# The last batch's values and keys beside the heads of the batch before it, and the first batch's gates among the second batch's front

## The chip, the cores and the metric

One core of a Trainium2 chip runs the program. The metric is the device time of one execution in microseconds (us); lower is better. The engines are PE (matrix products), DVE (vector), ACT (activations), POOL (GpSimd) and SP (it issues DMAs). Each works through its own list of instructions strictly in order, and they wait for one another through semaphores. PE reads SBUF and writes eight PSUM banks of 128x512 f32.

## The reference

`x` is 8 batches of 512 tokens with 128 channels, all f32. Each batch goes through two layers, each with two halves, every half a layer norm with scale and shift, then a residual add:

```
x += ga * attn0(norm(x))   # 16 heads, linear attention with elu, then a dense MLP with gelu
x += gb * moe(norm(x))     # 8 experts, each 128 -> 512 -> 128, silu(x Wg) * (x Wu) Wd
x += ga * attn1(norm(x))   # 8 causal heads of 16, softmax, within the 512 tokens
x += gb * switch(norm(x))  # 16 heads of 64, softmax over 512 tokens
# switch: gates Ws, Wd (16 heads x 8 experts), top 2 of 8 for each token and head
#   values v = sum of 2 experts' projections, weighted by sigmoid of the gate (mix_v)
#   q, k dense; attn = softmax(q k) v; result = sum over heads and 2 experts of attn @ Wo
```

The 512 tokens are four tiles of 128. Batches don't depend on each other.

## The kernel before

Each batch passes these stages, written on every engine as generators that yield "marks" (the count of marks in brackets):

- FRONT_A: `load` (1), `attn0` (24), `moe_in` (3): first layer's attention, MLP and the norm ahead of the experts. A long chain of short operations that hand over from engine to engine.
- `experts` (32): one mark for each block of 128 hidden units; three PE products, an ACT silu and a DVE product.
- FRONT_B: `attn1` (48, of which 35 are its 32 head tiles) and `gates` (13): the top-2 choice on `gate` with DVE and POOL on 128x1024 f32 tiles `eq`, `cand`, `oh1`, `oh2`; it ends in `mixv` (POOL) and `masko` (DVE).
- `values` (33): PE projects four tiles `pv` (experts' values) and eight blocks of `keys`; ACT copies them out of PSUM. 32 pieces then multiply `pv` with `mixv` into `prod` (three buffers, `NPROD`), and DVE sums each piece into `vals`. The products are shared between POOL and DVE: `VALUES_V` gives DVE every fourth, `LAST_VALUES_V` every second for the last batch. POOL's product n waits for the sum n-3; DVE's sum n waits for product n and stands one mark behind it.
- `begin` (2): the first two blocks of queries. `heads` (83): 64 head tiles and, between them, queries, `back`, `mixed` and `result` steps. For each pair of heads PE writes scores to banks S0 and S1, DVE takes the negated row maximum (`nmax`, L1520), ACT the exponential (`pr`, L1195), PE transposes into TB, ACT copies to `prT` (L1182), PE multiplies with `vals` into OB. `finish` (5) and `close` (4): the last tile's way through a DRAM round trip (`out_rows`, `onR`) to `xout` and the output DMA.

`schedule` merges two lists of marks for every engine alike: a main list, and a list beside it that is spread evenly over it (a mark of attn1's head tiles counts 1/4 to 1 by its width, the others 1, finish 1.6). `program` gives this order, with b the loop's batch:

1. FRONT_A(0); experts(0); FRONT_B(0); then FRONT_A(1) and experts(1) with values(0), begin(0) beside them.
2. Loop, six times: heads(b-1) with attn1(b), then gates(b) woven into FRONT_A(b+1) beside it; then experts(b+1) with finish(b-1), values(b), close(b-1), begin(b) beside it.
3. heads(6) with attn1(7), gates(7) beside; then finish(6), values(7), close(6), begin(7) with nothing beside; then heads(7), finish(7), close(7).

`arena` is a scratch tile of 128x6144 f32 that all stages up to attn1 share. `hdT` is the normed input of the switch layer, `hdB` its copy, made because the next front overwrites hdT; `xout` begins as a copy of `x5` for the like reason. values(b) uses banks TB, OB, S0, S1, which heads also use; the fronts and experts use F0 to F3.

Of the kernel before, what the change touches and what calls it, by code (L numbers as in the profile page):

```python
# [52 lines left out]
LAST_VALUES_V = [n for n in range(NQ * NT) if n % 2]  # L53


def values_v(b):
    return LAST_VALUES_V if isinstance(b[0], int) and sum(b) == NB - 1 else VALUES_V

# [47 lines left out]
CLOSE_BEHIND, BEGIN_BEHIND = 4, 28  # L106

# [17 lines left out]
def build(nc, a, row_table, out):  # L125
    ctx = ExitStack()
    with ctx:
# [104 lines left out]
        eq = sb("eq", [P, 2 * NT * HS, NE])[:, :, :]  # L232
        cand = sb("cand", [P, 2 * NT * HS, NE])[:, :, :]
        oh1 = sb("oh1", [P, 2 * NT * HS, NE])[:, :, :]
        oh2 = sb("oh2", [P, 2 * NT * HS, NE])[:, :, :]
# [9 lines left out]
        vals = sb("vals", [P, NT, HS, DS])  # L245
# [3 lines left out]
        keys = sb("keys", [P, NP, T])  # L249
# [17 lines left out]
        F0, F1, F2, F3, S0, S1, TB, OB = bank  # L267

# [133 lines left out]
        stage = vals[:, :, :, :].rearrange("p i h d -> p (i h d)")[:, 0:8 * T].rearrange("p (a t) -> p a t", a=8)  # L402
# [116 lines left out]
        def _(sp):  # L519
# [42 lines left out]
            def values(b):  # L562
                wait(sp, masko_r, b, 1)
                sp.dma_start(mask_rows.rearrange("(i p) c -> p i c", p=P), masko[:, :, :, :].rearrange("p i h e -> p i (h e)")).then_inc(mask_out[0], 16)
                yield CLOSE_BEHIND
                wait(sp, mask_out, b, 16)
                sp.dma_start(maskR[:, :, :], mask_rows.rearrange("(n t) (h e) -> (t h) n e", t=TG, e=NE)).then_inc(mask_in[0], 16)
                yield NQ * NT // 2
# [145 lines left out]
        def _(pe):  # L714
# [197 lines left out]
            def values(b):  # L912

                wait(pe, pT_r, b, 0)
                wait(pe, oa_r, b, 0)
                for n in range(NQ * NT):
                    if n == 0:
                        for i in range(2):
                            pe.matmul((TB, OB)[i][:, :], hdT[:, i * P:(i + 1) * P], WvT[:, :], start=True, stop=True).then_inc(pv_ps[0], 1)
                    if n % NQ == 0 and n // NQ in (1, 2):  # L920
                        i = n // NQ + 1
                        if i == 2:
                            wait(pe, s_out, b, 0)
                            wait(pe, xout_r, b, 0)
                        pe.matmul((S0, S1)[i % 2][:, :], hdT[:, i * P:(i + 1) * P], WvT[:, :], start=True, stop=True).then_inc(pv_ps[0], 1)
                    if n % 4 == 2:
                        p = n // 4
                        if p < 2:
                            wait(pe, hdB_r, b, 1)
# [3 lines left out]
                        pe.matmul((TB, OB)[p % 2][:, :], WkT[:, p * P:(p + 1) * P], hdB[:, :], start=True, stop=True).then_inc(k_ps[0], 1)  # L933
                    yield n + 1

            def begin(b):
                wait(pe, pv_r, b, NT)
# [24 lines left out]
            def steps(b, first, end):  # L962


                for k in range(first, end):
# [7 lines left out]
                    if kind == "queries":  # L973
                        for p in range(4):
                            last = pe.matmul(bank_k[:, p * P:(p + 1) * P], WqT[:, (4 * (x % 2) + p) * P:(4 * (x % 2) + p + 1) * P], hdB[:, (x // 2) * P:(x // 2 + 1) * P], start=True, stop=True)
# [29 lines left out]
                    if kind == "head":  # L1005
                        wait(pe, s_out, b, COPIED[k - 2])
                        if m >= 1:
# [24 lines left out]
        def _(s):  # L1032
# [105 lines left out]
            def values(b):  # L1138
                wait(s, vals_r, b, 0)
                for n in range(NQ * NT):  # L1140
                    if n == 0 or n % NQ == NQ // 2:
                        for i in (0, 1) if n == 0 else (n // NQ + 1,) if 1 <= n // NQ < NT - 1 else ():
# [3 lines left out]
                            s.activation(pv[:, i % 2, :], (TB, OB, S0, S1)[i][:, :], ACT.Copy).then_inc(pv_r[0], 1)  # L1146
                    if n % 4 == 3:
                        p = n // 4
                        wait(s, k_ps, b, p + 1)
                        s.activation(keys[:, p, :], (TB, OB)[p % 2][:, :], ACT.Copy).then_inc(keys_r[0], 1)  # L1150
                    if n == 0:
                        s.activation(hdB[:, :], hdT[:, :], ACT.Copy).then_inc(hdB_r[0], 1)
                    if n == NQ * NT // 2:
# [17 lines left out]
            def steps(b, first, end):  # L1171
                for k in range(first, end):
# [15 lines left out]
                    if kind == "head":  # L1188
# [4 lines left out]
                        if h == 0 and i >= 2:  # L1193
                            wait(s, rden_r, b, 2 * (i - 1))
# [16 lines left out]
        def _(v):  # L1211
# [257 lines left out]
            def values(b):  # L1469
                wait(v, mix_g, b, 3)  # L1470
                wait(v, oa_r, b, 0)
# [19 lines left out]
            def heads(b):  # L1491
                wait(v, xcopy_r, b, 1)
# [8 lines left out]
            def steps(b, first, end):  # L1501
                for k in range(first, end):
                    kind, m, _ = step_of(k - 1)
                    if kind == "result":
                        wait(v, s_ps, b, TURN[k - 1])
                        v.tensor_tensor(xout[:, m, :], (S0, S1)[TURN[k - 1] % 2][:, 0:P], xout[:, m, :], ALU.add).then_inc(xout_r[0], 1)
# [54 lines left out]
```

## Time and profile before

| | |
|---|---|
| median of 3 runs | 3037.46 us (3032.28 to 3060.35) |
| the profiled execution | 3036.23 us, of which 3034.4 us span from first to last instruction |
| PE busy | 2497.6 us, 82% of the span |
| DVE busy | 1565.5 us, 52% |
| ACT busy | 1361.4 us, 45% |
| POOL busy | 803.4 us, 26% |
| mean granted PE clock | 0.924 of 2.4 GHz |

The busy shares are means over stages with different limits; the profiled execution's own time is 1.8 us over its span, and 1.2 us under the median. A change in one stage is to be read from that stage's stretch of the trace.

### The profile page before, as it was taken

To read this page: it belongs to the slowest core of one execution; us is meant where nothing else is said; L and a number is where in the kernel's file an instruction comes from. 1 tells how busy PE (TensorE), PEld (TensorE's weight loads), DVE (VectorE), ACT (ScalarE), POOL (GpSimd) and SP (SyncE) were. 2 spreads that over 40 slices of the span, in tenths; PEclk is the share of its full clock that TensorE was granted. 3 is DMA by queue.
4 is the path that set the end of the run, shared out by engine and by line. 5 is a ranking of instruction groups with operands and counts; after the bars stand their busy time and mean duration, and the time that the engine had idled before them with its cause. 6 is when DMAs were issued, how large, how long until landed. Compare 5 with 4: busy or idle time off the path is not lost.

```text
span 3034.4 us, 45348 instructions
## 1 busy us (share of the span) xinstructions
PE 2497.6 (82%) x15660; PEld 1535.7 (51%) x15660; DVE 1565.5 (52%) x2646; ACT 1361.4 (45%) x2925; POOL 803.4 (26%) x370
## 2 busy tenths in 40 slices
PE   3984699879897898889898798978988898986476
PEld 2353346554475445654365544754456544754254
DVE  4235753456635484464835565364834557337632
ACT  0232226463364525554265634555255633643254
POOL 1002620015501191013700164011900147004500
PEclk7996799999899998999899998999989999998798
DMA  2110010102010030102101030101201121001001
GB/s 75 42 49 9 9 54 1 50 22 67 22 38 20 25 78 2 43 28 47 44 1 56 15 77 12 43 15 43 60 2 43 29 56 33 15 15 40 0 29 32
DMA packets 210741, 101.69 MB, mean 34 GB/s; under 512 B 137369, under 2 KB 189622, under 8 KB 210494
## 3 DMA queue, kind: packets, MB, share of 16 engines
q1 hardware_dynamic: 205052, 95.74, 11.4%
q10 hardware_dynamic: 5440, 2.75, 0.3%
q8 instruction: 143, 2.34, 0.3%
q14 instruction: 106, 0.85, 0.1%
HBM read 77.48 MB, written 20.99 MB: 32 GB/s over the span
## 4 chain that ended last, share of the span: by engine, by line
issue 42%; PE 34%; POOL 10%; DVE 7%; ACT 6%; DMA 1%; ACTq 0%; POOLq 0%; DVEq 0%
POOL prod L702 7%; PE bank L717 6%; PE bank L984 5%; PE bank L829 4%; PE bank L832 4%; PE bank L1021 3%; PE bank L837 3%; ACT prT L1182 2%; ACT pr L1195 2%; POOL rstd L641 1%; PE bank L869 1%; DVE nrm_o L1294 1%; PE bank L996 1%; DVE prod L1477 1%; PE bank L885 1%
## 5 line engine op out<-in xcount | busy, mean ns | idle before, releaser
L702 POOL TENSOR_TENSOR prod<-pv,mixv 128x1024 f32<-128x1024 f32 x184 | 608.3, 3344 | 243.3 <-ACT pv L1146 170.5
L1520 DVE TENSOR_REDUCE nmax<-bank 128x1 f32<-128x512 f32 x512 | 340.6, 687 | 608.1 <-PE bank L984 605.6
L1182 ACT ACTIVATE prT<-bank 128x512 f32<-128x512 f32 x512 | 305.6, 597 | 611.2 <-PE bank L717 607.3
L984 PE MATMUL bank<-keys,qs 64*128 64x512 f32 x1024 | 318.0, 698 | 220.1 <-ACT pr L1195 92.4
L641 POOL TENSOR_TENSOR rstd<-vareps,minus_half 128x4 f32<-128x4 f32 x48 | 50.0, 1042 | 1323.7 <-DVE vareps L1289 1323.6
L1195 ACT ACTIVATE pr<-bank,nmax 128x512 f32<-128x512 f32 x512 | 349.5, 685 | 98.3 <-DVE nmax L1520 97.3
L717 PE MATMUL bank<-ident,pr 128*128 128x128 f32 x2048 | 351.7, 298 | 36.1 <-ACT prT L1182 35.9
L717 PEld LDWEIGHTS bank<-ident,pr 128*128 128x128 f32 x2048 | 241.8, 150 | 270.1 <-issue 217.1
L1088 ACT ACTIVATE arena<-bank 128x512 f32<-128x512 f32 x256 | 152.8, 597 | 469.3 <-PE bank L829 429.4
L1021 PE MATMUL bank<-prT,vals 128*64 128x128 f32 x4096 | 299.5, 292 | 63.0 <-ACT prT L1182 63.0
L1485 DVE TENSOR_REDUCE vals<-prod 128x128 f32<-128x1024 f32 x256 | 306.6, 1208 | 35.9 <-POOL prod L702 35.9
L1378 DVE TENSOR_TENSOR arena<-bank,arena 128x512 f32<-128x512 f32 x256 | 175.1, 686 | 245.2 <-PE bank L832 230.9
L1021 PEld LDWEIGHTS bank<-prT,vals 128*64 128x64 f32 x4096 | 235.8, 145 | 115.4 <-ACT prT L1182 72.7
L832 PE MATMUL bank<-h1T,Wu 128*128 128x512 f32 x512 | 268.4, 606 | 19.0 <-DVE arena L1378 19.0
L1406 DVE TENSOR_REDUCE nmax<-bank 128x1 f32<-128x128 f32 (+3 forms) x256 | 125.7, 491 | 282.9 <-PE bank L870 282.2
L829 PE MATMUL bank<-h1T,Wg 128*128 128x512 f32 x512 | 266.2, 602 | 0.9 <-ACT h1T L1053 0.9
L837 PE MATMUL bank<-arena,Wd 128*128 128x512 f32 x512 | 263.6, 600 | 2.8 <-DVE arena L1378 2.4
L984 PEld LDWEIGHTS bank<-keys,qs 64*128 64x128 f32 x1024 | 84.3, 197 | 281.3 <-ACT pr L1195 113.2
L869 PE MATMUL bank<-arena,attT 128*128 128x512 f32 (+3 forms) x512 | 198.9, 473 | 4.4 <-ACT arena L1116 3.0
L1477 DVE TENSOR_TENSOR prod<-pv,mixv 128x1024 f32<-128x1024 f32 x72 | 179.7, 2495 | 0.0
L832 PEld LDWEIGHTS bank<-h1T,Wu 128*128 128x128 f32 x512 | 97.6, 193 | 147.1 <-issue 113.2
L885 PEld LDWEIGHTS bank<-v,arena 128*128 128x128 f32 x1280 | 165.8, 194 | 1.0 <-issue 1.0
(220 smaller groups left out, 3077.1 us busy)
## 6 DMA issues: line engine op xcount, KB each, us to landing
Wg<-in_L_ffn_Wg SPq DMA_DIRECT2D x64, 256.0 KB, 2.8
Wu<-in_L_ffn_Wu SPq DMA_DIRECT2D x64, 256.0 KB, 3.1
Wd<-in_L_ffn_Wd SPq DMA_DIRECT2D x64, 256.0 KB, 3.8
out_rows<-on SPq DMA_DIRECT2D x32, 512.0 KB, 2.6
onR<-out_rows SPq DMA_DIRECT2D x32, 512.0 KB, 3.8
xin<-in_L_attn_x SPq DMA_DIRECT2D x8, 256.0 KB, 4.2
mask_rows<-masko SPq DMA_DIRECT2D x8, 256.0 KB, 4.3
maskR<-mask_rows SPq DMA_DIRECT2D x8, 256.0 KB, 6.6
```

The costliest lines, as they stand in the source:

```text
L702: g.tensor_tensor(*value_piece(n), ALU.mult).then_inc(vprod_r[0], 1)
L717: last = pe.transpose(dst[:, i * P:(i + 1) * P], src(i), ident[:, :])
L829: pe.matmul(F0[:, :], Wg[:, e % 2, j * P:(j + 1) * P], hbT[:, :], start=True, stop=True).then_inc(gu_g[0], 1)
L832: pe.matmul((F2, F3)[n % 2][:, :], Wu[:, e % 2, j * P:(j + 1) * P], hbT[:, :], start=True, stop=True).then_inc(gu_u[0], 1)
L837: pe.matmul(F1[:, :], Wd[:, e % 2, j, :], act[:, m % 3, :], start=(m == 0), stop=(m == n_all - 1)).then_inc(down_ps[0], 1)
L869: pe.matmul(f[:, 0:w], q1T[:, i * P:(i + 1) * P], k1z[:, h, 0:w], start=True, stop=False, skip_group_check=True)
L984: pe.matmul((S0, S1)[(turn + odd) % 2][:, :], qs[half, j % 3, r, :], keys[half, p, :], start=True, stop=True).then_inc(s_ps[0], 1)
L1021: last = pe.matmul(OB[DS * odd:DS * odd + DS, at:at + P], vals[:, j, h - 1 + odd, :], prT[:, (m - 1 + odd) % 3, j * P:(j + 1) * P], start= ...
L1182: s.activation(prT[:, m % 3, :], TB[:, :], ACT.Copy).then_inc(pT_r[0], 1)
L1195: s.activation(pr[:, x % 2, :], bank_k[:, :], ACT.Exp, bias=nmax[:, x % 2:x % 2 + 1], accum_out=den[:, i % 2, h:h + 1]).then_inc(s_out[0], 1)
L1485: v.tensor_reduce(vals[:, i, HQ * q:HQ * q + HQ, :], prod[:, m % NPROD, :].rearrange("p (h d e) -> p h d e", h=HQ, e=NE), X_AXIS, ALU.add) ...
L1520: v.tensor_reduce(nmax[:, m % 2:m % 2 + 1], (S0, S1)[turn % 2][:, :], X_AXIS, ALU.max, negate=True).then_inc(nmax_r[0], 1)
```

## The change

The last batch's values and keys get memory and banks of their own, so that values(7) can run while heads(6) still read theirs: `vals` of batch 7 lies in arena[0:4096], which attn1 of that batch has by then left; `keys` of batch 7 lies in the memory of eq, cand, oh1, oh2 (now one tile `picks`), free once masko and mixv are made. The products go to banks F0 to F3. The copies hdB and xout are left out for that batch. DVE's share of its products falls from 16 to 10 of 32. In `program`, marks 1 to 24 of values(7) stand behind attn1(7) and gates(7) beside heads(6), 25 to 28 beside finish(6), 29 to 32 beside close(6), mark 33 with begin(7). At the start, gates(0) is woven into FRONT_A(1) behind attn1(0), with nothing beside, and values(0), begin(0) stand beside experts(1) alone.

```
-LAST_VALUES_V = [n for n in range(NQ * NT) if n % 2]
+LAST_VALUES_V = [n for n in range(NQ * NT) if n % 3 == 2]
+LAST_BESIDE = 24
-        vals = sb("vals", [P, NT, HS, DS])
-        keys = sb("keys", [P, NP, T])
+        vals_last = arena[:, 0:NT * HS * DS].rearrange("p (i h d) -> p i h d", i=NT, h=HS)
+        keys_last = picks[:, :, :, :].rearrange("p k n e -> p (k n e)").rearrange("p (a t) -> p a t", a=NP)
...
-                              (of(FRONT_B, 0), []), (of(FRONT_A, 1) + of(("experts",), 1), of(("values", "begin"), 0))])
+                              (fronts(0), []), (of(("experts",), 1), of(("values", "begin"), 0))])
...
-            schedule(stages, [(of(("heads",), last - 1), of(FRONT_B, last)),
-                              (after_heads(last, -1), []), (of(("heads", "finish", "close"), last), [])])
+            at = (last, 0)
+            schedule(stages, [(of(("heads",), last - 1), of(FRONT_B, last) + [("values", at, range(1, LAST_BESIDE + 1))]),
+                              (of(("finish",), last - 1), [("values", at, range(LAST_BESIDE + 1, LAST_BESIDE + CLOSE_BEHIND + 1))]),
+                              (of(("close",), last - 1), [("values", at, range(LAST_BESIDE + CLOSE_BEHIND + 1, MARKS["values"]))]),
+                              (of(("begin",), last) + [("values", at, [MARKS["values"]])], []),
+                              (of(("heads", "finish", "close"), last), [])])
...
+                if is_last(b):
+                    A, B, C, D, of_hd = F0, F1, F2, F3, hdT
+                    wait(pe, gate_r, b, 2)
+                else:
+                    A, B, C, D, of_hd = TB, OB, S0, S1, hdB
...
             def begin(b):
-                wait(pe, pv_r, b, NT)
+                if is_last(b):
+                    wait(pe, s_out, b, 0)
+                    wait(pe, xout_r, b, 0)
+                    wait(pe, oa_r, b, 0)
+                else:
+                    wait(pe, pv_r, b, NT)
...
+                        if p == 0 and is_last(b):
+                            wait(s, masko_r, b, 1)
+                            wait(s, mix_g, b, 3)
...
             def heads(b):
-                wait(v, xcopy_r, b, 1)
+                if is_last(b):
+                    wait(v, stored, b, 0)
+                else:
+                    wait(v, xcopy_r, b, 1)
```

## Rows read from the trace of the kernel before

**Rows 1.** Windows: width; busy (count) PE, PEld, DVE, ACT, POOL; PE clock; DMA share; GB/s

```profile
284.00:361.00 77.00, 31.93 (x83) 17.27 (x84) 61.61 (x99) 12.54 (x21) 52.14 (x22) 0.66 0.06 4
361.00:450.00 89.00, 88.98 (x220) 39.55 (x218) 47.05 (x52) 24.80 (x41) 27.79 (x11) 1.00 0.17 54
2447.00:2555.00 108.00, 103.91 (x336) 47.98 (x335) 79.54 (x76) 31.85 (x54) 81.38 (x25) 0.98 0.24 62
2767.00:2848.00 81.00, 28.63 (x152) 16.57 (x147) 74.11 (x54) 11.80 (x22) 70.48 (x17) 0.63 0.13 24
```

**Rows 2.** Timeline of DVE: front(0) begins; gates(0); front(1) begins; heads(0) begin

```profile
42.79 0.87 DVE L1281 BATCH_NORM_STATS2 stats<-xin 128x6 f32<-128x128 f32 x4 [5.41 <-DMA rows<-row_table]
...
263.15 1.22 DVE L1434 TENSOR_REDUCE top<-gate 128x128 f32<-128x1024 f32 x1 [6.55 <-ACT gate L1130]
...
284.56 0.17 DVE L1300 TENSOR_SCALAR modA<-mod 128x12 f32<-128x12 f32 x1 [3.22 <-POOL mixv L692]
...
450.42 0.69 DVE L1520 TENSOR_REDUCE nmax<-bank 128x1 f32<-128x512 f32 x1 [2.88 <-PE bank L984]
```

**Rows 3.** Timeline of PE: the first Wg product of experts(0) and (1)

```profile
94.67 2.08 PE L829 MATMUL bank<-h1T,Wg 128*128 128x512 f32 x2 [0.93 <-ACT h1T L1053]
...
360.58 1.06 PE L829 MATMUL bank<-h1T,Wg 128*128 128x512 f32 x1
```

**Rows 4.** Timeline of DVE: a norm's four tiles in batch 0's, then batch 1's front

```profile
91.46 1.11 DVE L1294 TENSOR_SCALAR nrm_o<-h,mv,rstd 128x128 f32<-128x128 f32 x4 [1.13 <-POOL rstd L641]
...
323.96 8.06 DVE L1294 TENSOR_SCALAR nrm_o<-h,mv,rstd 128x128 f32<-128x128 f32 x4 [1.12 <-POOL rstd L641]
```

**Rows 5.** L1520's busy us (count), PE clock, in windows of heads(5), (6), (7)

```profile
2207.50:2338.00 130.50, 20.89 (x31) 0.94 0.08 25
...
2720.20:2766.70 46.50, 10.73 (x18) 0.85 0.08 24
2847.60:2925.90 78.30, 19.94 (x32) 0.96 0.05 15
2925.90:2958.20 32.30, 7.13 (x13) 1.00 0.12 33
2958.20:3011.00 52.80, 13.55 (x21) 0.97 0.07 21
2969.00:3011.00 42.00, 10.35 (x17) 0.96 0.09 26
```

**Rows 6.** Products in 2447:2555, then 2787:2848: duration ns min/median/max, first, last start

```profile
L702 POOL TENSOR_TENSOR prod<-pv,mixv x24: 2822/2856/4497, 2465.9 to 2546.2; 128x1024 f32<-128x1024 f32 x24
...
L1477 DVE TENSOR_TENSOR prod<-pv,mixv x8: 1926/2772/3309, 2473.3 to 2549.0; 128x1024 f32<-128x1024 f32 x8
...
L702 POOL TENSOR_TENSOR prod<-pv,mixv x13: 4332/4350/4406, 2787.6 to 2839.4; 128x1024 f32<-128x1024 f32 x13
...
L1485 DVE TENSOR_REDUCE vals<-prod x29: 1197/1207/1216, 2786.3 to 2846.5; 128x128 f32<-128x1024 f32 x29
```

**Rows 7.** Timeline of one pair of heads of batch 7

```profile
2972.15 1.29 DVE L1520 TENSOR_REDUCE nmax<-bank 128x1 f32<-128x512 f32 x2 [2.50 <-PE bank L984]
...
2974.68 0.68 ACT L1195 ACTIVATE pr<-bank,nmax 128x512 f32<-128x512 f32 x1
```

**Rows 8.** Timeline of DVE: heads(6) begin; its tail; heads(7) begin; its tail

```profile
2555.02 0.69 DVE L1520 TENSOR_REDUCE nmax<-bank 128x1 f32<-128x512 f32 x1 [1.22 <-PE bank L984]
...
2774.22 4.43 DVE L1477 TENSOR_TENSOR prod<-pv,mixv 128x1024 f32<-128x1024 f32 x1
...
2847.61 0.68 DVE L1520 TENSOR_REDUCE nmax<-bank 128x1 f32<-128x512 f32 x1
3010.41 1.29 DVE L1520 TENSOR_REDUCE nmax<-bank 128x1 f32<-128x512 f32 x2 [1.28 <-PE bank L984]
...
3017.96 0.69 DVE L1514 TENSOR_TENSOR on<-bank,rden 128x512 f32<-128x512 f32 x1 [4.75 <-PE bank L988]
...
3031.50 0.29 DVE L1506 TENSOR_TENSOR xout<-bank,xout 128x128 f32<-128x128 f32 x1 [11.72 <-PE bank L1002]
```

More of the change, by code:

```diff
@@ L52, with is_last @@
 VALUES_V = [n for n in range(NQ * NT) if n % 4 == 3]
-LAST_VALUES_V = [n for n in range(NQ * NT) if n % 2]
+LAST_VALUES_V = [n for n in range(NQ * NT) if n % 3 == 2]
+def is_last(b):
+    return isinstance(b[0], int) and sum(b) == NB - 1
 def values_v(b):
-    return LAST_VALUES_V if isinstance(b[0], int) and sum(b) == NB - 1 else VALUES_V
+    return LAST_VALUES_V if is_last(b) else VALUES_V
 def by_pool(n, by_v):
@@ L231, in build @@
         gate = sb("gate", [P, 2, NT, HS, NE])
[L232 to L235, printed above, removed]
+        picks = sb("picks", [P, 4, 2 * NT * HS, NE])
+        eq, cand, oh1, oh2 = (picks[:, k, :, :] for k in range(4))
         top = sb("top", [P, 2, 2 * NT * HS])
@@ L267, in build, with vals_of, keys_of @@
         F0, F1, F2, F3, S0, S1, TB, OB = bank
+        def vals_of(b):
+            return vals_last if is_last(b) else vals_loop
+        def keys_of(b):
+            return keys_last if is_last(b) else keys_loop
         def tiles(t):
@@ L564, in values @@
                 sp.dma_start(mask_rows.rearrange("(i p) c -> p i c", p=P), masko[:, :, :, :].rearrange("p i h e -> p i (h e)")).then_inc(mask_out[0], 16)
-                yield CLOSE_BEHIND
+                yield MARKS["values"] - 1 if is_last(b) else CLOSE_BEHIND
                 wait(sp, mask_out, b, 16)
                 sp.dma_start(maskR[:, :, :], mask_rows.rearrange("(n t) (h e) -> (t h) n e", t=TG, e=NE)).then_inc(mask_in[0], 16)
-                yield NQ * NT // 2
+                if not is_last(b):
+                    yield NQ * NT // 2
                 wait(sp, xout_r, b, 0)
@@ L918, in values @@
                         for i in range(2):
-                            pe.matmul((TB, OB)[i][:, :], hdT[:, i * P:(i + 1) * P], WvT[:, :], start=True, stop=True).then_inc(pv_ps[0], 1)
+                            pe.matmul((A, B)[i][:, :], hdT[:, i * P:(i + 1) * P], WvT[:, :], start=True, stop=True).then_inc(pv_ps[0], 1)
                     if n % NQ == 0 and n // NQ in (1, 2):
                         i = n // NQ + 1
-                        if i == 2:
+                        if i == 2 and not is_last(b):
                             wait(pe, s_out, b, 0)
                             wait(pe, xout_r, b, 0)
-                        pe.matmul((S0, S1)[i % 2][:, :], hdT[:, i * P:(i + 1) * P], WvT[:, :], start=True, stop=True).then_inc(pv_ps[0], 1)
+                        pe.matmul((C, D)[i % 2][:, :], hdT[:, i * P:(i + 1) * P], WvT[:, :], start=True, stop=True).then_inc(pv_ps[0], 1)
                     if n % 4 == 2:
@@ L928, in values @@
                         if p < 2:
-                            wait(pe, hdB_r, b, 1)
+                            if not is_last(b):
+                                wait(pe, hdB_r, b, 1)
                             wait(pe, pv_r, b, p + 1)
@@ L932, in values @@
                             wait(pe, keys_r, b, p - 1)
[L933 removed]
+                        pe.matmul((A, B)[p % 2][:, :], WkT[:, p * P:(p + 1) * P], of_hd[:, :], start=True, stop=True).then_inc(k_ps[0], 1)
                     yield n + 1
             def begin(b):
[L937 removed]
+                if is_last(b):
+                    wait(pe, s_out, b, 0)
+                    wait(pe, xout_r, b, 0)
+                    wait(pe, oa_r, b, 0)
+                else:
+                    wait(pe, pv_r, b, NT)
                 yield from steps(b, 0, BEGIN)
@@ L974, in steps @@
                         for p in range(4):
-                            last = pe.matmul(bank_k[:, p * P:(p + 1) * P], WqT[:, (4 * (x % 2) + p) * P:(4 * (x % 2) + p + 1) * P], hdB[:, (x // 2) * P:(x // 2 + 1) * P], start=True, stop=True)
+                            last = pe.matmul(bank_k[:, p * P:(p + 1) * P], WqT[:, (4 * (x % 2) + p) * P:(4 * (x % 2) + p + 1) * P], hd[:, (x // 2) * P:(x // 2 + 1) * P], start=True, stop=True)
                         last.then_inc(s_ps[0], 1)
@@ L1149, in values @@
                         wait(s, k_ps, b, p + 1)
-                        s.activation(keys[:, p, :], (TB, OB)[p % 2][:, :], ACT.Copy).then_inc(keys_r[0], 1)
-                    if n == 0:
+                        if p == 0 and is_last(b):
+                            wait(s, masko_r, b, 1)
+                            wait(s, mix_g, b, 3)
+                        s.activation(keys[:, p, :], (A, B)[p % 2][:, :], ACT.Copy).then_inc(keys_r[0], 1)
+                    if n == 0 and not is_last(b):
                         s.activation(hdB[:, :], hdT[:, :], ACT.Copy).then_inc(hdB_r[0], 1)
-                    if n == NQ * NT // 2:
+                    if n == NQ * NT // 2 and not is_last(b):
                         wait(s, stored, b, 0)
@@ L1192, in steps @@
                         i, h = x // HS, x % HS
-                        if h == 0 and i >= 2:
-                            wait(s, rden_r, b, 2 * (i - 1))
+                        if h == 0 and (i >= 2 or i == 0 and is_last(b)):
+                            wait(s, rden_r, b, max(0, 2 * (i - 1)))
                         s.activation(pr[:, x % 2, :], bank_k[:, :], ACT.Exp, bias=nmax[:, x % 2:x % 2 + 1], accum_out=den[:, i % 2, h:h + 1]).then_inc(s_out[0], 1)
@@ L1469, in values @@
             def values(b):
+                vals = vals_of(b)
                 wait(v, mix_g, b, 3)
-                wait(v, oa_r, b, 0)
+                if not is_last(b):
+                    wait(v, oa_r, b, 0)
                 for n in range(NQ * NT + 1):
```

17 lines of the change are left out of this document (11 added, 6 removed).

## Prediction

> **What bounds the kernel now.** I read first which stretches leave PE idle: the windows by stage. PE is filled beside the experts of a loop turn (104 of 108 us), but there are two thin places [rows 1]. From 284 to 361 us, where values(0) stand beside FRONT_A(1), PE works 32 of 77 us; from 2767 to 2848 us, where values(7) stand alone, 29 of 81, while DVE works 74 and POOL 70. The timeline says why the first is long. FRONT_A alone takes 51.9 us for batch 0, from its first statistics (42.79) to the first Wg product (94.67); for batch 1 it takes 76.0 (284.56 to 360.58) [rows 2, 3]. One norm took 8.06 us beside POOL's products where it takes 1.11 [rows 4]. The change attacks both places and leaves the six turns of the loop alone, so everything is decided by two differences.
>
> **The start.** Before, the gates' first reduction starts at 263.15 and the second front at 284.56, 21.4 us later; the first Wg product is at 360.58 and the first maximum of heads(0) at 450.42 [rows 2, 3]. After, one reduction (1.22) and one comparison of the same width stand ahead of the front's statistics, so it begins near 265.6. The front then needs 51.9. Of the gates' DVE work nine steps are left, each near the 1.22 of the first, about 10.5 us in all, strewn between the front's marks. As the front alone leaves DVE idle for most of its 51.9, I charge half: 5. POOL's cand and mixv products can still catch a norm, but none is caught by the values' products any more. First Wg product: 265.6 + 51.9 + 5 = 322.5, against 360.6. Bounds for the 5: 0 and 21.4 (all the gates' own length, as if nothing overlapped).
>
> The experts then carry all 32 pieces, not about half. Before, with that half, they take 89.8 us from first Wg product to first maximum [rows 2, 3]. What moves in is about six pairs of PE products of 0.86 us a pair (some 103 pairs' worth of work fill the 89 us of the window [rows 1]): 95 us. The other bound is a loop turn, 108 us, with all values but also the rest of heads(b-1), and it starts its POOL products 19 us after its window begins [rows 1, 6]. POOL's 24 products took 2465.9 to 2549.1 there, 83 us, so they fit [rows 6]. I take 99. First maximum: 322.5 + 99 = 421.5 against 450.4, so **-29 us** (bounds: -41 and -3).
>
> **The end, heads(6).** The old stretch from the first maximum of heads(6) to the first of heads(7) is 2555.0 to 2847.6, 292.6 us [rows 5, 8]. I cut the new heads(6) where `schedule` changes what is beside: attn1(7) now ends at mark 40 of 83 (it was 60), the gates fill marks 41 to 55, values marks 56 to 82; mark 41 is the 32nd head, mark 56 the 43rd.
> 1. To the 32nd head: attn1 is spread as in a loop turn (mark 38), so a loop turn's time, 130.5 us [rows 5].
> 2. To the 43rd: alone 32.3. The gates added 46.5 - 42.0 = 4.5 over the last 17 heads of heads(6) [rows 5]; 37 in sum.
> 3. To the last: alone 52.8 [rows 5]. Added to DVE: 24 sums at 1.21 and 8 products at about 2.5 (between the shortest, 1.93, and the median, 2.77, beside POOL), 49 us [rows 6], onto about 18 of its own (13.55 for the maxima, the rest `on` and `spread`). So no less than 67. The added PE work is four and six pairs at 0.86, 9 us, and ACT's are ten copies of about the length of an exponential, 0.68 [rows 7]. How much is hidden I read from one pair of heads: the maxima end at 2973.44, the second exponential starts at 2974.68, so a wait of 1.2 us between the two maxima is free, and DVE is idle 2.5 us before the next pair [rows 7]. A sum of 1.2 hides in either place; a sum with a product (3.7) costs 2.5 in the one and about 1 in the other: 8 x 1.75 = 14. For PE's 9 I charge 5, for ACT's copies 3, for the start of the values (mixv, then pv) 2. In sum 52.8 + 24 = 77 us (bounds: 67, and 111 if DVE's and PE's whole addition lies on the path).
>
> Heads(6): 130.5 + 37 + 77 = 244 us where they took 211.7 (2555.0 to 2766.7) [rows 5, 8].
>
> **The end, from heads(6) to heads(7).** Without values the tail of a batch takes 3011.7 to 3031.8, 20.1 us, the last maximum's end to xout's [rows 8]. Before `on` three value marks stand on DVE (three sums, one product, 5.7 us) against the 4.75 that DVE waits there anyway: +1.5 with the products' lateness. The next three fall into the 12.8 us from the end of `on` to xout, which hold the DRAM round trip: nothing. Then begin(7), which now waits for xout: two blocks of queries, their copies, the scores: I take 5.5 us, two blocks and one pair of scores of 1.1 us at full clock and 2.1 at half, as the first Wg pair was at 94.67 and 360.58 [rows 3], less what overlaps. SP's order puts the store ahead of maskR and rows1b, and DVE's new wait on `stored` (two batches share xout, the store takes under 3 us) ends inside these 5.5. In sum 27 us, where it was 80.9 (2766.7 to 2847.6); bounds 24 and 38.
>
> Together 244 + 27 = 271 against 292.6: **-21.5 us** (bounds -34 and +24). Heads(7) and its tail keep their 186.8 us. PE's clock was 0.63 in the stretch that goes, 0.96 behind it [rows 1, 5], so heads(7) might start at a higher clock: 0 to 2 us of gain, of which I take none. TensorE: Matmul & The Clock Gate of the Trainium skill (Part 1) says the same in general: an idle array falls to 1.2 GHz and must be kept busy to return to 2.4; by it alone the new tail of 27 us would still end at the low clock and nothing would be gained.
>
> **The sum.** 3036.2 - 29 - 21.5 = 2985.7 for a profiled execution; these stand 1.2 under the median, so 2987 us.
>
> **The rivals.**
> - The lock. POOL's products took 2.86 us in the loop's median and 4.35 where each met a DVE product, and one DVE product took 4.43 [rows 6, 8]. If each of the 8 DVE products in heads(6) waits for POOL's running one to that length, they cost 8 x 1.9 = 15 us more: 3002. For it: POOL will be nearly always busy. Against: the loop's median is 2.77. The Trainium skill (SBUF — State Buffer, Who interferes with whom) makes it a rule: the port pair that DVE and GpSimd share is locked for a whole instruction, and the second fully blocks. By that rule the 15 us come in full and this change is the place for them; the loop's rows bear out only half.
> - The gates don't weave. Each gates step on DVE waits for POOL, and the front stands behind it; the front then ends near 263 + 21.4 + 52 = 336.5, 14 us later: 3001. Against: in the front DVE idles most of the time.
> - DVE in series. Its 49 us and PE's 9 in heads(6) lie wholly on the path: +34, 3021. For: in-order DVE, whose maxima release every exponential. Against: the idle 2.5 us of [rows 7].
> - Slower: a convoy. If POOL can't run ahead, each value mark costs DVE a whole POOL product before its sum, 4.35 + 1.21, with the next maxima behind it: 24 x 5.56 = 133 on top of 52.8, 109 more than my 77: 3096. It decides from some 80 us more than I take, where all gains are gone and 1% is lost. Against: three buffers, and POOL's 16 products fill only 16 x 2.85 + 8 x 1.9 = 61 us of 77.
> - The change doesn't do what it says: the values start no earlier, because mixv(7) is late. Then the end gives 0: 3008. Against: gates end at mark 55 by the schedule.
>
> **How the numbers follow.** Forecast (2974 to 3000) 0.53; better than that (clock, cheaper hiding) 0.11; the lock or unwoven gates (about 3000 to 3007) 0.15; in series or a late mixv (3008 to 3025) 0.16; convoy 0.05. The measurement tells 1%, 30 us, from no change, so faster means under 3007: 0.53 + 0.11 + 0.15 = 0.79; within 1% 0.17; slower 0.04. The range 2971 to 3014 leaves out about two cases in ten.
>
> **What would show it.** In the changed kernel: the first Wg product of experts(1) near 322 and the first maximum of heads(0) near 421; heads(6) 244 us from first to last maximum with 77 behind the 43rd, DVE almost full there; 27 us from its last to the next first maximum; the loop's turns unchanged. I am wrong if POOL's products leave DVE waiting within heads(6) (idle ended by L702), if the front stays over 65 us, or if experts(1) take over 105.

## The result and the profile after

The changed kernel takes 2995.2 us in the median of 4 runs (2992.25 to 3007.38), the kernel before 3035.4 of 4 in the same session: 0.9874 of it, 95% interval 0.9828 to 0.9921, so 0.8 to 1.7% faster. The forecast was 2987, range 2971 to 3014. The profiled execution took 2994.33 us with a span of 2992.5.

The windows by stage of the changed kernel, columns as in [rows 1]; the first three stand against [rows 1], the next three are heads(6) up to its 32nd, 43rd and last maximum, then its tail, then heads(7):

```profile
266.00:328.00 62.00, 28.34 (x73) 15.90 (x73) 35.08 (x91) 9.28 (x17) 14.56 (x11) 0.58 0.06 7
328.00:429.00 101.00, 98.93 (x236) 43.78 (x236) 81.58 (x73) 29.82 (x50) 76.57 (x25) 0.98 0.16 49
...
2522.90:2647.10 124.20, 109.80 (x887) 80.67 (x888) 49.09 (x109) 73.14 (x173) 6.46 (x7) 0.97 0.03 10
2647.10:2686.20 39.10, 29.30 (x264) 19.82 (x263) 21.60 (x28) 19.86 (x48) 8.19 (x5) 0.92 0.12 34
2686.20:2775.80 89.60, 60.01 (x412) 35.92 (x412) 66.80 (x61) 33.82 (x79) 49.77 (x18) 0.83 0.04 12
2775.80:2803.50 27.70, 17.48 (x128) 13.22 (x124) 18.47 (x17) 5.23 (x10) 16.98 (x5) 0.62 0.33 57
2803.50:2969.10 165.60, 125.96 (x1144) 82.73 (x1144) 50.40 (x83) 86.96 (x209) 1.27 (x1) 0.96 0.07 21
```

The stretch in which values(7) stood alone, 81 us with PE 29 us busy [rows 1], is a tail of 27.7. What it was has moved into the third line of heads(6): PE 60 of 89.6 us, DVE 66.8, at a granted clock of 0.83. The start is two lines now: a front of 62 us with POOL all but idle, then experts that fill PE again, 98.9 of 101.

The timeline of DVE and, for L848, of PE, with the marks of the sums (against [rows 2, 3, 8]):

```profile
266.07 1.22 DVE L1470 TENSOR_REDUCE top<-gate 128x128 f32<-128x1024 f32 x1 [6.55 <-ACT gate L1161]
...
304.20 3.13 DVE L1330 TENSOR_SCALAR nrm_o<-h,mv,rstd 128x128 f32<-128x128 f32 x4 [1.12 <-POOL rstd L660]
...
324.76 1.11 DVE L1330 TENSOR_SCALAR nrm_o<-h,mv,rstd 128x128 f32<-128x128 f32 x4 [1.14 <-POOL rstd L660]
...
428.80 0.69 DVE L1561 TENSOR_REDUCE nmax<-bank 128x1 f32<-128x512 f32 x1 [4.53 <-PE bank L1015]
```
```profile
327.97 2.07 PE L848 MATMUL bank<-h1T,Wg 128*128 128x512 f32 x2 [0.93 <-ACT h1T L1084]
```

The second of these rows is the norm of batch 1's front that took 8.06 us before [rows 4]. Its counterpart in batch 0's front is not the 1.11 of [rows 4] but this row of the kernel before:

```profile
71.53 3.13 DVE L1294 TENSOR_SCALAR nrm_o<-h,mv,rstd 128x128 f32<-128x128 f32 x4 [1.12 <-POOL rstd L641]
```

So that norm is back at the length it has there. The four norms of this kind (L1294, now L1330) together took 21.0 us in batch 1's front before (3.54, 3.56, 8.06, 5.85) and take 8.5 now (1.11, 3.13, 3.13, 1.11); the first 3.13 is the one that still meets a product of the gates on POOL (L698, 2.34 us).

| stretch | before | forecast | after |
|---|---|---|---|
| gates' first reduction to first Wg product of experts(1) | 97.4 | 59.4 | 61.9 |
| from there to the first maximum of heads(0) | 89.8 | 99 | 100.8 |
| heads(6) to the 32nd maximum | 107.5 | 130.5 | 124.2 |
| to the 43rd | 39.6 | 37 | 39.1 |
| to the last | 64.6 | 77 | 89.6 |
| last maximum to the first of heads(7) | 80.9 | 27 | 27.7 |
| heads(7) and its tail | 186.8 | 186.8 | 189.0 |

By these rows the start gives 24.5 us and heads(6) with its tail 12.0; heads(7) takes 2.2 more. That is 34 of the 42 us between the two spans (3034.4 and 2992.5). The gates begin 2.9 us later (266.07 against 263.15), before any changed instruction, and the stretch from the first maximum of heads(0) to that of heads(6), whose instructions are the same, was 10.5 shorter (2104.6 and 2094.1). The last section comes back to that.

In the third line of heads(6) the longest waits in total were those of ACT's copies for PE's transposes (41.7 us). The rivals are told apart by the following (who waited, for whom: us in total, times, longest), and these are the lengths of DVE's products there (min/median/max):

```profile
POOL prod L721 <- DVE arena L1523: 34.1, 11, 5.2
...
ACT pr L1231 <- DVE nmax L1561: 13.7, 7, 2.6
...
DVE arena L1523 <- POOL prod L721: 4.1, 1, 4.1
```
```profile
L1515 DVE TENSOR_TENSOR prod<-pv,mixv x8: 1919/2936/4231, 2692.7 to 2772.9; 128x1024 f32<-128x1024 f32 x8
```

It is POOL that waits for DVE's sums, 34 us, not DVE for POOL (4.1, once): no convoy. ACT's exponentials wait 13.7 us for maxima that stand behind values on DVE. One place of the timeline shows how:

```profile
2713.27 1.21 DVE L1523 TENSOR_REDUCE arena<-prod 128x128 f32<-128x1024 f32 x1
...
2714.62 2.82 POOL L721 TENSOR_TENSOR prod<-pv,mixv 128x1024 f32<-128x1024 f32 x1 [1.64 <-DVE arena L1523]
...
2714.99 4.21 DVE L1515 TENSOR_TENSOR prod<-pv,mixv 128x1024 f32<-128x1024 f32 x1
...
2720.25 0.67 DVE L1561 TENSOR_REDUCE nmax<-bank 128x1 f32<-128x512 f32 x1
```

A sum frees a buffer, POOL starts its next product in that moment, DVE's own product comes 0.37 us behind it and takes 4.21 us where the shortest took 1.92. The next maximum begins at 2720.25, behind that product and its sum; its scores had ended at 2717.5. Three of the eight products began 0.37 us behind one of POOL's and took 4.16 to 4.23; two met what was left of one (1.56 and 0.86 us) and took 3.25 and 2.63; three met none and took 1.92 to 1.94. In each of the five that met one, the length is what was left of POOL's product plus 1.7 to 1.8 us.

### The profile page after: what moved, and what is told of

It reads as the page before. It is cut to its first block and busy times, and to the rows that moved or that the text cites. A ratio compares the mean times of both kernels' runs of the same rounds, so it can differ in the third digit from the quotient of the medians.

```text
span 2992.5 us, 45343 instructions
## 1 busy us (share of the span) xinstructions
PE 2503.9 (84%) x15660; PEld 1542.3 (52%) x15660; DVE 1556.1 (52%) x2640; ACT 1361.7 (46%) x2923; POOL 802.5 (27%) x376
## 3 DMA queue, kind: packets, MB, share of 16 engines
q1 hardware_dynamic: 205052, 95.74, 11.4%
## 5 line engine op out<-in xcount | busy, mean ns | idle before, releaser
L1015 PE MATMUL bank<-keys,qs 64*128 64x512 f32 x896 | 279.6, 702 | 191.6 <-ACT pr L1231 61.5
L736 PE MATMUL bank<-ident,pr 128*128 128x128 f32 x2048 | 353.5, 299 | 35.5 <-ACT prT L1218 35.5
L1052 PE MATMUL bank<-prT,vals 128*64 128x128 f32 x3584 | 264.5, 293 | 47.5 <-ACT prT L1218 47.5
L1523 DVE TENSOR_REDUCE vals<-prod 128x128 f32<-128x1024 f32 x224 | 269.3, 1209 | 42.5 <-POOL prod L721 42.5
L848 PE MATMUL bank<-h1T,Wg 128*128 128x512 f32 x512 | 266.9, 603 | 2.3 <-ACT h1T L1084 2.3
L1052 PEld LDWEIGHTS bank<-prT,vals 128*64 128x64 f32 x3584 | 208.2, 146 | 94.3 <-ACT prT L1218 61.8
L1015 PEld LDWEIGHTS bank<-keys,qs 64*128 64x128 f32 x896 | 73.4, 197 | 246.2 <-ACT pr L1231 81.2
L1141 ACT ACTIVATE arena<-bank 128x128 f32<-128x128 f32 (+3 forms) x256 | 112.1, 438 | 123.7 <-PE bank L736 122.9
```

The lines of the kernel that those rows point to most:

```text
L736: last = pe.transpose(dst[:, i * P:(i + 1) * P], src(i), ident[:, :])
L848: pe.matmul(F0[:, :], Wg[:, e % 2, j * P:(j + 1) * P], hbT[:, :], start=True, stop=True).then_inc(gu_g[0], 1)
L1015: pe.matmul((S0, S1)[(turn + odd) % 2][:, :], qs[half, j % 3, r, :], keys[half, p, :], start=True, stop=True).then_inc(s_ps[0], 1)
L1052: last = pe.matmul(OB[DS * odd:DS * odd + DS, at:at + P], vals[:, j, h - 1 + odd, :], prT[:, (m - 1 + odd) % 3, j * P:(j + 1) * P], start= ...
L1523: v.tensor_reduce(vals[:, i, HQ * q:HQ * q + HQ, :], prod[:, m % NPROD, :].rearrange("p (h d e) -> p h d e", h=HQ, e=NE), X_AXIS, ALU.add) ...
```

## The experiments

All lengths are from the profiled execution, for heads(6) cut at the 32nd, 43rd and last maximum as above. "Third stretch" is the last of these.

**The start alone.** Only the start's lines of `program` are the changed ones.

```
# the kernel before, with
-   (of(FRONT_B, 0), []), (of(FRONT_A, 1) + of(("experts",), 1), of(("values", "begin"), 0))])
+   (fronts(0), []), (of(("experts",), 1), of(("values", "begin"), 0))])
```

> Only the start is changed: gates(0) woven into FRONT_A(1), values(0) and begin(0) beside experts(1); the end is the kernel before's. If the start's gain is the order of that stretch, the first Wg product of experts(1) is near 326 us, the first maximum of heads(0) near 427 where it was 450, the stretch from the first maximum of heads(6) to that of heads(7) stays at 292.6, and the time is about 3012. Rival: most of the 22 us seen at the start is lost again when the loop takes over (heads(0) meets late transfers or buffers); then the first maximum of heads(1) is no more than 10 us earlier and the time is over 3025.

3015.8 us (5 runs), 0.9941 of before (0.9924 to 0.9959). The first Wg product came at 328.8, the first maximum of heads(0) at 429.2, that of heads(1) 22.8 us earlier than before, and from the first maximum of heads(6) to that of heads(7) it took 292.8. The gain stays: the new order of the start, with the end as before, is worth about 20 us.

**The end alone.** The changed kernel with the old start.

```
# the changed kernel, with
-   (fronts(0), []), (of(("experts",), 1), of(("values", "begin"), 0))])
+   (of(FRONT_B, 0), []), (of(FRONT_A, 1) + of(("experts",), 1), of(("values", "begin"), 0))])
```

> Only the end is changed: values(7) beside heads(6); the start is the kernel before's. If the two parts add, the stretch from the first maximum of heads(6) to that of heads(7) is 280 us as in the changed kernel (292.6 before), of it 90 behind the 43rd head, and the time is about 3024, a gain of 12. Rival: the end alone gives the 21 that I had worked out, and the loop's jitter hid it in the changed kernel; then the stretch is 271 and the time 3014.

3031.7 us (10 runs, four from 3015 to 3024 and six from 3030 to 3038), 0.9981 (0.9960 to 1.0001). In the profiled one (3030.2) the stretch was 284.4 us, not 280.6, and heads(7) took 169.5, not 165.6. The first of these differences is in the second part of heads(6), 44.3 us where the changed kernel has 39.1 with the same instructions:

```profile
2675.20:2719.50 44.30, 34.51 (x264) 22.93 (x262) 21.60 (x27) 19.92 (x48) 8.59 (x5) 0.77 0.10 30
```

The granted clock was 0.77 there and 0.92 in the changed kernel; DVE and ACT did the same work in the same time, PE took 5.2 us more. The third stretch was 88.3 us at a clock of 0.83, much as in the changed kernel. So the rival (a stretch of 271 us, 21 gained) is out; this execution shows 8 us gained at the end, and the medians 3.5. Whether the two parts add can't be told from the medians: 19.4 and 3.5 us, together 40, each with an interval some 10 us wide or more.

**All products on POOL.** DVE keeps the sums.

```
-LAST_VALUES_V = [n for n in range(NQ * NT) if n % 3 == 2]
+LAST_VALUES_V = []
```

> The changed kernel, but POOL makes all 32 products of the last batch (DVE made 10). Theory A (DVE's order): the stretch behind the 43rd head of heads(6), 89.6 us, is long because sums and above all products stand between DVE's maxima, and a DVE product waits for POOL's running one; without the 8 products (23 us of DVE) it falls to about 75, and the time to about 2981. Theory B (POOL's supply): DVE waits for products, so with 8 more of them on POOL (24 x 2.85 = 68 us and its waits for buffers) the stretch grows to 95 or more and the time to 3000. Theory C (PE's work and its low clock): neither matters, 88 to 91.

2979.1 us (4 runs), 0.9813 (0.9786 to 0.9839). The third stretch fell from 89.6 to 70.0 us, the parts ahead of it stayed (124.2 and 39.1):

```profile
2694.50:2764.60 70.10, 52.65 (x405) 31.44 (x406) 44.34 (x54) 33.01 (x78) 68.09 (x25) 0.93 0.06 16
```

DVE has 22.5 us less to do and the stretch is 19.6 shorter, though POOL has more: theory A, and 5 us further than it said. PE is busy 7.4 us less for nearly the same work (405 products, not 412), at a clock of 0.93 instead of 0.83, so part of the 19.6 may have come through the clock. The clock goes with the order of the work here and not with the single execution: 0.83 in all three profiles of the changed end, 0.93 in both with all on POOL. How much of the 19.6 is DVE's time alone no run separates. POOL is now busy for 68.1 of 70.1 us; that it is the next bound is likely, not shown (see the spread values below).

**Five buffers.** The buffers four and five of the last batch's products lie in arena[4096:6144].

```
+LAST_NPROD = 5
...
+            k, size = n % nprod(b), HS * NE * DS // NQ
+            return prod[:, k, :] if k < NPROD else arena[:, 4096 + (k - NPROD) * size:4096 + (k - NPROD + 1) * size]
...
-                        if n >= NPROD:
-                            wait(g, vals_r, b, n - NPROD + 1)
+                        if n >= nprod(b):
+                            wait(g, vals_r, b, n - nprod(b) + 1)
```

> The changed kernel, but the last batch's products have five buffers (two in arena behind attn1's probabilities) where it has three. POOL stood idle 34 us in the stretch behind the 43rd head, waiting for DVE's sums to free a buffer. Theory A (DVE's order): that idleness costs nothing, the stretch stays at 88 to 91 us, only POOL's waits move. Theory B (POOL's supply): with room to run ahead POOL is never late and the stretch falls to about 80.

One execution, 2986.0 us. The third stretch is 86.0 us, 3.6 less and under the 88 to 91 of theory A, but far from B's 80; in two other kernels with the changed end it was 88.3. The tail, 25.4, is 2.3 less, but with no edit near it the tail also took 24.8 (gates not woven). DVE's eight products changed too: they took 18.0 us together instead of 24.3 (mean 2.25), three of them met one of POOL's, not five. So this run took away both POOL's lateness and most of the collisions, and gained 3.6 us at most.

```profile
2685.10:2771.10 86.00, 59.11 (x416) 34.56 (x416) 62.29 (x62) 33.69 (x79) 52.26 (x19) 0.86 0.04 13
```

**Both.** All on POOL, five buffers.

```
-LAST_VALUES_V = [n for n in range(NQ * NT) if n % 3 == 2]
+LAST_VALUES_V = []
...
+LAST_NPROD = 5
```

> All products of the last batch on POOL and five buffers. With POOL alone the stretch behind the 43rd head of heads(6) was 70.0 us, with five buffers alone 86.0 (89.6 in the changed kernel). If the two gains are of one kind (DVE is late and POOL with it) five buffers give little more: 68 to 70, time about 2978. If they add, 66 and below, time about 2973, unless POOL's 16 more products of 2.85 become the bound: 24 pieces x 2.85 = 68 us, then 70 again.

2982.9 us (4 runs), 0.9832 (0.9816 to 0.9849); third stretch 69.9, POOL busy 67.9 of it. The gains don't add: with all products on POOL, room to run ahead is worth nothing. The 68 to 70 expected for the stretch held, the time was 5 us over the 2978 expected, and the third stretch of 70 came twice.

**The gates not woven.** The start's front as in the kernel before, the values as in the changed one.

```
-   (fronts(0), []), (of(("experts",), 1), of(("values", "begin"), 0))])
+   (of(FRONT_B, 0) + of(FRONT_A, 1), []), (of(("experts",), 1), of(("values", "begin"), 0))])
```

> The changed kernel, but gates(0) stand ahead of FRONT_A(1), not woven into it; values(0) stay beside experts(1). If weaving gives what I charged for it, the first Wg product of experts(1), 61.9 us after the gates' first reduction in the changed kernel, comes 21.4 + 52 = 73 to 75 us after it, 12 us later. Rival: the gain was only that POOL's products no longer meet the front's norms, and weaving gives nothing: 60 to 64 us.

One execution, 3009.1 us. From the gates' first reduction (263.21) to the first Wg product (337.72) it took 74.5 us, 12.6 more than woven. With the values beside it, unwoven, it was 97.4 [rows 2, 3]. So of the 35.5 us by which this front became shorter 22.9 came from taking the values away and 12.6 from the weaving; the values cost 10 to 11 back beside the experts (89.8 to 100.8 in the changed kernel, 100.2 here). Net, from the gates' first reduction to the first maximum, taking the values away gave 12.5 us (187.2 to 174.7) and the weaving 12.0 (174.7 to 162.7). The four norms took 6.5 us here where they took 21.0: about 14.5 of the 22.9.

**Sums made twice.** DVE makes the first 16 sums of batch 7 a second time, into scratch.

```
+                        if is_last(b) and m < 16:
+                            v.tensor_reduce(arena[:, 4096 + 128 * m:4096 + 128 * m + 128].rearrange("p (h d) -> p h d", h=HQ), prod[:, m % NPROD, :].rearrange("p (h d e) -> p h d e", h=HQ, e=NE), X_AXIS, ALU.add)
```

> The changed kernel, in which DVE makes the first 16 sums of batch 7 twice (the second copy goes to unused scratch): 16 x 1.21 = 19.4 us of DVE more, in pieces of 1.2 that I had forecast to hide between the maxima. If sums hide, the stretch behind the 43rd head stays within 5 us of 89.6. If DVE's work there lies on the path whatever its kind, as the 19.6 us gained for 23.5 us of products suggest, it grows by 0.8 of 19.4, to 105.

One execution, 3006.0 us. The third stretch grew from 89.6 to 103.0, DVE's busy time in it by 16.9 (66.8 to 83.7; its products had fewer long ones):

```profile
2687.90:2790.90 103.00, 66.14 (x418) 37.57 (x416) 83.67 (x77) 33.92 (x79) 49.73 (x18) 0.77 0.04 11
```

13.4 for 19.4 us: short pieces of DVE's work don't hide here either. PE was busy 6.1 us longer, at 0.77 instead of 0.83, so here too part of the length may have come through the clock. A likely reading is that the free 1.2 us between two maxima is taken by the first sum already; no run tests the first sums alone.

**POOL's products cut to a corner.** POOL's products of batch 7 cover 128x64 of 128x1024 elements, the rest of that work is left out; all of DVE's is made.

```
-                        g.tensor_tensor(*value_piece(n), ALU.mult).then_inc(vprod_r[0], 1)
+                        piece = [x[:, 0:1, 0:8, :] for x in value_piece(n)] if is_last(b) else value_piece(n)
+                        g.tensor_tensor(*piece, ALU.mult).then_inc(vprod_r[0], 1)
```

> The changed kernel, but POOL makes only a 128x64 corner of each of its products of batch 7, so it leaves out most of that work and of its use of SBUF; the values are not those of the reference. This takes away both POOL's lateness (3.6 us by the five buffers) and its collisions with DVE's eight products (2.94 us mean, 1.93 alone: 8 us). If those two are all, the stretch falls from 89.6 to about 78, still well over the 70 of the run without DVE products: the products' plain length is then the larger part. If the lock is the whole of the matter, it falls to 70 or below.

One execution, 2981.6 us. The third stretch and DVE's eight products:

```profile
2686.90:2761.80 74.90, 54.04 (x413) 32.60 (x412) 58.08 (x62) 33.80 (x79) 7.88 (x18) 0.92 0.05 15
```
```profile
L1516 DVE TENSOR_TENSOR prod<-pv,mixv x8: 1909/1938/1962, 2691.0 to 2758.8; 128x1024 f32<-128x1024 f32 x8
```

I had expected about 78 if lateness and collisions were all, 70 or below if the lock was the whole of the matter; it was 74.9. With POOL out of the way the added work of DVE, PE and ACT holds heads(6) up by 22 us (52.8 alone to 74.9); POOL's presence costs the other 14.7. Each of the eight products takes 1.94, not 3.03 in the mean: 8.7 us less of DVE's time, measured directly. The split of the 14.7 stays open: the five buffers' 3.6 can't be added to the 8.7, since that run had 6.3 of the 8.7 in it, and PE was busy 6.0 us less here at a clock of 0.92, not 0.83.

**Values spread over more heads.** Five buffers, all on POOL, and a weight of 1.5 for the last batch's value marks in the merging order; then the same with every sixth product on DVE; then the weight alone on the changed kernel.

```
-def weight(name, m):
+def weight(name, m, b):
...
-    return (1 + min((m - A1 - 1) // H1, NT - 1)) / NT if name == "attn1" and A1 < m <= E1 else FINISH_SHARE if name == "finish" else 1
+    return LAST_WEIGHT if name == "values" and is_last(b) else (1 + min((m - A1 - 1) // H1, NT - 1)) / NT if name == "attn1" and A1 < m <= E1 else FINISH_SHARE if name == "finish" else 1
```

> Five buffers, all products on POOL, and each value mark of the last batch counts 1.5 in the merging order, so attn1(7) and gates(7) end sooner (near mark 48 of 83) and the values spread over some 27 heads that take about 70 us alone, not 21 that take 53. With POOL's 24 x 2.85 = 68 us the bound of the old stretch (67.9 busy of 69.9 us), it should no longer bound: heads(6) 224 us where it took 233.2, the time 2972. Rival: attn1 pushed into fewer heads costs what the values save: 233 again, 2981.

> As the run before, with DVE making every sixth product. If POOL's supply still matters when spread, heads(6) gets 2 to 3 us shorter than without the share; if DVE's order is what is left, the four products within heads(6) cost 0.7 to 0.8 of their 2.4 us each, 7 to 8 us more.

> The changed kernel with the weight of 1.5 alone (three buffers, DVE makes every third product). DVE's added 50 us stand among 27 heads, not 21. If what counts is DVE's length in the order (0.7 to 0.8 of it lands on the path wherever it stands), heads(6) stays near 253 us. If it counts by how full DVE gets in a stretch (67 of 89.6 us), it hides better among more heads: 240 to 245.

The first: 2982.4 us (5 runs), 0.9819 (0.9797 to 0.9841), the same as without it. Heads(6) took 240.6 us, not 224, and more than the rival's 233: to the 32nd maximum 132.6 where it was 124.1, and the third stretch 69.5 as before, though POOL was busy for only 59.0 of it. The tail was 4 us shorter (23.2). So the direction of the rival held, attn1 in fewer heads costs more than the values save. And a third stretch that stays at 69.5 with a POOL that has 9 us less to do speaks against POOL as its only bound; what else holds it at 70 is open. The share (one execution, 2984.6) changed heads(6) by -0.8 us, neither the 2 to 3 less nor the 7 to 8 more expected, and its tail was 27.5, 4.3 longer. The weight alone (one execution, 3002.4) gave 261.3 us for heads(6), 8 more than the changed kernel, where I expected 253 or 240 to 245: 11.4 more before the 32nd maximum, 3.9 more before the 43rd, 6.9 less behind it. The cost lies ahead, most likely in attn1 and the gates, which stand beside fewer heads; whether DVE's work hides better among more heads this doesn't tell.

**Three products on DVE.** Five buffers, and:

```
-LAST_VALUES_V = [n for n in range(NQ * NT) if n % 3 == 2]
+LAST_VALUES_V = [7, 15, 23]
```

> The changed kernel with five buffers and only three of the last batch's products on DVE (pieces 7, 15, 23, all beside heads(6)). With all on POOL it was busy 67.9 of the 69.9 us behind the 43rd head, so it bounds; three products on DVE take 3 x 2.85 = 8.6 us off it and put 3 x 2.2 us on DVE, of which 0.7 to 0.8 lands on the path: 5 us. If both hold, the stretch is 53 + 16 + 5 less what POOL cost, 68 to 71, no gain over 69.9, and the time near 2980: the optimum is flat. Rival: POOL's supply costs more than DVE's order here, and the stretch is 66 or less, the time 2975.

2991.1 us (6 runs, 2971 to 3009), 0.9838 (0.9803 to 0.9874). The third stretch was 80.0, far over the 68 to 71, and went at a clock of 0.85 where it was 0.93 with all on POOL; the part ahead of it, in which no edit differs from the changed kernel, took 44.4 us at 0.77:

```profile
2696.90:2776.80 79.90, 59.36 (x416) 36.41 (x415) 54.36 (x57) 34.06 (x79) 68.75 (x24) 0.85 0.05 14
```

DVE has 10 us more than with all on POOL (54.4 against 44.3): its three products, of 3.14, 4.22 and 2.46 us, each of which met one of POOL's. They made the stretch 10 us longer, all of their length, where I had expected 5 for them less what POOL gave back. The low clock ahead is not the reason: with the end alone and with the gates not woven the part ahead went at 0.77 too (44.3 us), and the third stretch was 88.3 where it is 89.6 behind 0.92. It is one profile, PE was busy 6.8 us longer in the stretch, and the runs spread over 38 us, so what three products cost at an equal clock stays open. That the optimum is flat is not borne out.

## Why the prediction was right, point by point

**The start.** Forecast -29, measured -24.5 in the stretch; the start alone is faster by its own interval, 12 to 23 us, which confirms the gain and not its full size. The front came out at 61.9, not 59.4: the charge of 5 us for the woven gates was 2.5 short. The experts with all values took 100.8, not 99. The rival that gates don't weave would have given 73; unwoven gave 74.5, which shows its price (12.6) as well as that it didn't happen. The reason given for the long front was right, but [rows 4] overstates it: the 8.06 us norm takes 3.13 in batch 0's front, not 1.11, and it is the 5.85 us one that takes 1.11 there. And the bound of -41 doesn't follow from its own terms: 0 us for the gates and 95 for the experts give -38.

**Heads(6) to the 32nd.** I took a loop turn's 130.5 and it was 124.2. The loop's turn runs that part at a clock of 0.94 [rows 5], this one at 0.97; a turn of the changed kernel's loop again took 130.6 at 0.94. The clock was not in my sum, and neither was the work: a loop turn holds the whole of attn1 and the first marks of what follows in that part, 900 PE products, the new heads(6) 887. Spread values had 900 there and took 132.6 at 0.97. So the 6.3 us are mostly my choice of a fuller part as the model, not luck with the clock: the new end took 124.0 to 124.2 in all nine profiles that have this order.

**The third stretch.** This is the term that was mis-sized: 52.8 + 24 = 77, measured 89.6. The sum of DVE's work was right (no less than 67; 66.8 busy). What failed is the price put on DVE's added work beside POOL. I took 2.5 us for a product and let part of it hide; it was 3.03 in the mean, 4.2 us more over the eight, and the stretch was 12.6 over. With POOL all but out of the way the stretch took 74.9, where my own rule, with products of 1.94 (8 x 1.3 on the path, not 8 x 1.75), gives about 73. So the hiding comes out right in sum there, though one part of it, the free sums, is contradicted below; that the two agree may be errors that cancel.

The first rival, the lock, was priced at 15 us over the forecast: each of the eight products was to wait to 4.4 us. As a mechanism it is shown, in its size it isn't. Three of eight waited nearly that long (4.16 to 4.23), two waited in part, three not at all, because POOL was itself waiting for buffers (34 us); over the forecast's 2.5 a product that is 4.2 us of DVE's time, not 15. The 12.6 and the 14.7 of POOL's presence look like the rival's 15 and hold something more: POOL's lateness and PE's lower clock are the candidates, and no run divides them. The time is nearer the forecast than this stretch because other terms ran the other way: the loop was 10.5 us shorter, which was luck, and the first part of heads(6) 6.3. Without these two the sum of the rows would have been 3012, just inside the range.

The Trainium skill's rule (SBUF — State Buffer, Who interferes with whom), that the second of the two engines fully blocks for the first one's whole instruction, agrees with the 4.21 us row: 2.45 us of POOL's product were left when DVE's began, and 2.45 + 1.92 = 4.37. It agrees with the other four that met one within 0.3 us as well. What the rule doesn't say is how often the two meet, and that is what the price hung on.

**Hiding sums.** I had let sums of 1.2 us go for nothing, between two maxima or before the next pair. Sixteen more cost 13.4, so where one sum already stands a second isn't free.

**The tail** (27 against 27.7) was right, though within it the 1.1 us for a pair at full clock is misread: the 360.58 row of [rows 3] is a single product of 1.06 us, at half clock like the pair at 94.67. It has hardly any weight in the 5.5. **The convoy** didn't come (DVE waited 4.1 us for POOL, once). DVE in series would have given a third stretch of 111. **Heads(7)** was to stay at 186.8 and took 189.0; its clock is 0.96 where it was 0.97, behind a tail at 0.62, so the higher clock that I had left out of the sum gave nothing, and one longer run of it (169.5) was seen with the end alone, so I don't put a cause to 2 us.

**The total** was 8 us off (2987 against 2995): +4.3 at the start, +12.6 in the third stretch, +2.1, +0.7 and +2.2 in the rest, -6.3 in the first part of heads(6), and -10.5 in the loop, by the clock: PE was busy 1830.8 us there instead of 1841.8 for the same work, DVE, ACT and POOL within 2 us of before. The remaining 3 are the later start of the gates, which from one kernel to the next came anywhere from 262.6 to 268.3. That the total is only 8 off owes as much to these offsets as to the terms.

**A better version.** With all of the last batch's products on POOL the median is 2979.1 (0.9813, 0.9786 to 0.9839) against 2995.2 (0.9874, 0.9828 to 0.9921) for the change as it was made. The intervals of the two ratios overlap by a hair; the third stretch, 70.0 and 69.9 us in two kernels against 89.6, 88.3 and 88.3 in three, is the firmer evidence.

## What to carry to other kernels

When work moves beside a chain that hands over through one in-order engine, count what it adds to that engine and put most of it on the path (here 0.7 to 0.9 of each us, the change of PE's clock that came with it included); idle gaps between its instructions hide little. Give the partner engine the whole of the work that both could do when it has the time: a product on DVE cost more than the same product on POOL, since it held up the maxima and met POOL's on the way. And take a chain of short steps, like a front or a norm, out of reach of an engine that contends with it: at the start that gave 22.9 us in the front, of which the displaced work took 10 back behind it, so that net it was worth as much as the weaving (12 us each).

## What the runs showed of the hardware

The same instructions take different times between the 32nd and the 43rd maximum, and the granted clock goes with it. Two turns of the loop in the kernel before, heads(1) and heads(4), columns as in [rows 1]:

```profile
932.10:972.40 40.30, 32.51 (x273) 21.72 (x273) 24.86 (x60) 19.91 (x48) 4.34 (x3) 0.84 0.09 27
1989.80:2026.90 37.10, 29.40 (x272) 20.14 (x273) 24.80 (x60) 19.75 (x48) 4.34 (x3) 0.95 0.10 30
```

DVE, ACT and POOL agree to 0.2 us; PE is busy 3.1 us longer at 0.84 than at 0.95. Heads(6) of the changed end, which holds other instructions there, took 39.1 us at 0.92 and 44.3 at 0.77, PE's busy time 29.3 and 34.5. PE was busy for 75 to 81% of these stretches. Where in such a stretch it gets 1.2 and where 2.4 GHz differs between turns and between profiles whose instructions there are the same. Over the six turns of the loop, whose instructions no edit changed, the 14 profiles took from 2093.3 to 2104.6 us, 11 us apart, about the spread that the runs of one kernel have. An edit worth less than that is better read from its own stretch, with the clock beside it, than from the time.

A DVE product with both inputs in SBUF (128x1024 f32, 1.92 to 1.94 us where it met none of POOL's) that starts while POOL's product of the same size runs takes what is left of POOL's plus 1.7 to 1.8 us, up to 4.23. The other way round, POOL's product took 4.36 us instead of 2.8 when it began 1.5 us behind DVE's that had itself been held up. With POOL's products cut to a corner all eight of DVE's took 1.91 to 1.96.
